# Macaron block, float32, one core: four normalisations on VectorE, the values product at the end of a step, the turned h and h2n in another PSUM bank, SyncE's moves in another order

## What is computed

```python
x = x + 0.5 * ffn_stack(layernorm(x))   # 2 layers: shift_token, qkv of 8 heads of 64,
                                        # l2norm(q), l2norm(k), rotary xpos, attention over
                                        # the own and the previous window of 64, @ wo, residual;
                                        # shift_token, layernorm, w1, a * gelu(g), w2, residual
x = x + attn(layernorm(x))              # z = y @ W for k, q, v; each layernormed with gain and
                                        # bias; softmax(k @ q.T) @ v, over all 1024 tokens; + y
x = x + 0.5 * ffn_stack(layernorm(x))
```

## Time and profile before

| | us |
|---|---|
| median of three runs | 1809.63 (1808.24 to 1811.32) |
| the profiled execution | 1811.45 |
| its span, first to last instruction | 1809.7 |
| granted TensorE clock, mean of the span | 0.967 |

### The profile page before, as it was taken

The page is one execution under the profiler, slowest core; times in us unless marked ns, Lnnn a source line. Parts: engine busy times, 40 slices in busy tenths (PEclk is TensorE's granted clock), DMA queues, the critical chain, the costliest instruction groups (busy, mean ns, idle before and its releaser), DMA issues.

```text
span 1809.7 us, 44041 instructions
## 1 busy us (share of the span) xinstructions
PE 1523.7 (84%) x15864; PEld 1237.8 (68%) x15864; DVE 1323.5 (73%) x3420; ACT 1174.8 (65%) x2460; POOL 1098.1 (61%) x1130
## 2 busy tenths in 40 slices
PE   1789999978999999867878979999998899999984
PEld 1677777766777777754656757777776777777763
DVE  6687879777788887754434469797977687979772
ACT  1576767666677776745565567676766576767671
POOL 3685858576677676633232168585857576858560
PEclk9999999999999999988889989999999999999996
DMA  8241212231312131113100142122223131212113
GB/s 282 49 123 39 59 46 57 55 86 45 77 42 57 40 80 40 41 50 97 35 12 24 33 104 53 44 53 50 55 58 89 41 77 41 58 47 54 44 28 118
DMA packets 183670, 112.46 MB, mean 62 GB/s; under 512 B 86720, under 2 KB 164128, under 8 KB 182944
## 3 DMA queue, kind: packets, MB, share of 16 engines
q1 hardware_dynamic: 183456, 109.65, 23.2%
HBM read 43.41 MB, written 23.42 MB: 37 GB/s over the span
## 4 chain that ended last, share of the span: by engine, by line
PE 51%; DVE 26%; ACT 9%; issue 7%; SPq 3%; DMA 2%; POOL 1%; DVEq 0%; ACTq 0%; POOLq 0%
PE QK L388 10%; PE TO L638 9%; PE QK L638 5%; PE TO L705 5%; DVE rope_c L1136 5%; DVE rope_s L1141 4%; DVE o_n L1161 4%; PE TO L388 3%; DVE top L1080 3%; PE SC L679 3%; DVE h2n L1148 3%; PE TO L807 2%; PE VB L807 2%; PE TO L751 2%; ACT probs L1278 2%
## 5 line engine op out<-in xcount | busy, mean ns | idle before, releaser
L1278 ACT ACTIVATE probs<-SC,shift,qgain 128x128 f32<-128x128 f32 x1024 | 389.7, 480 | 102.2 <-DVE shift L1088 101.9
L1472 POOL TENSOR_TENSOR ve<-mv,epsilon 128x1 f32<-128x1 f32 x128 | 24.3, 190 | 393.4 <-DVE mv L1127 393.4
L388 PE MATMUL QK<-w_qkv,hT 128*128 128x512 f32 x768 | 223.7, 429 | 23.4 <-DMA w_qkv<-qkv_d 10.9
L1136 DVE TENSOR_TENSOR rope_c<-QK,rope 128x512 f32<-128x512 f32 x256 | 175.7, 686 | 81.5 <-PE QK L388 79.0
L1485 POOL TENSOR_TENSOR rnorm<-clip,mhalf 128x8 f32<-128x8 f32 x128 | 210.9, 1647 | 13.1 <-DVE clip L1097 13.1
L1494 POOL TENSOR_TENSOR qgain<-clip,mhalf 128x8 f32<-128x8 f32 x128 | 209.3, 1635 | 0.0
L638 PE MATMUL TO<-ident,probs 128*128 128x128 f32 x1280 | 188.7, 274 | 20.8 <-ACT probs L1278 11.2
L1272 ACT ACTIVATE v_own<-VB 128x512 f32<-128x512 f32 x128 | 76.5, 598 | 191.1 <-PE VB L388 191.1
L1080 DVE TENSOR_REDUCE top<-SC 128x4 f32<-128x512 f32 x256 | 174.6, 682 | 28.8 <-PE SC L679 28.5
L1141 DVE TENSOR_TENSOR rope_s<-QK,rope 128x256 f32<-128x256 f32 x512 | 190.9, 415 | 0.0
L638 PEld LDWEIGHTS TO<-ident,probs 128*128 128x128 f32 x1280 | 152.4, 141 | 54.8 <-issue 34.3
(11 more groups left out here) (170 smaller groups left out, 3760.8 us busy)
## 6 DMA issues: line engine op xcount, KB each, us to landing
v_prev<-v_own SPq DMA_DIRECT2D x256, 130.0 KB, 2.3
x_att<-stream SPq DMA_DIRECT2D x128, 64.0 KB, 2.3
h<-stream SPq DMA_DIRECT2D x256, 32.0 KB, 1.9
stream<-x_new SPq DMA_DIRECT2D x32, 256.0 KB
w_qkv<-qkv_d SPq DMA_DIRECT2D x3, 1536.0 KB, 6.8
h<-x_mid SPq DMA_DIRECT2D x128, 32.0 KB
h<-x_mid SPq DMA_DIRECT2D x128, 31.8 KB
rope<-rope_d SPq DMA_DIRECT2D x24, 128.0 KB, 3.2
```

The costliest lines, as they stand in the source:

```text
L388: last = mm(dst, fr(left(a)), fr(right(b)), start=(k == 0), stop=(k == 2))
L1136: v.tensor_tensor(qk(rope_c[:])[:, m], src, rope[:, i, m, 0:1, :].to_broadcast([P, HEADS, DH]), ALU.mult)
L1278: last = nc.scalar.activation(probs[:, b, hd, :], SC[:, hd * P:hd * P + P], ACT.Exp, bias=shift[:, b, hd:hd + 1], scale=qgain[:, b, hd % 4 ...
```

## The change

- In the preparation of the attention, y's and z's key and query normalisations move from ScalarE to VectorE (eight `tensor_scalar` with mean and rstd each). GpSimd computes only variance plus epsilon and rstd for them (`rstd_of`). The value part stays on ScalarE (`v_normalised`), at stage 7 instead of 8. On VectorE the row's maximum moves ahead of the last of z's additions and its statistics.
- In a stack's step TensorE does the v projection after h's and h2n's turning, before o_n's. h and h2n are turned into the first columns of TT instead of VB. Before the first four probabilities are turned, TensorE waits for s_hl and s_h2l of the step before; the burst's first pair waits for both as well.
- VectorE does the low parts of hT and h2T before the sum of squares.
- ScalarE copies v_own between h2T and oT.
- SyncE moves x_mid into h2 first and v_own into v_prev after that.

```diff
@@ moves, SyncE
-                if t := tile(QKV):
-                    need(sp, s_vown, t.count())
-                    sp.dma_start(v_prev[0:64, k, :], v_own[0:64, k, :]) ...
                 if t := tile(WO):
                     need(sp, s_xm, t.count())
                     sp.dma_start(h2[:, k, 0:64], x_mid[:, i, 0:64]) ...
+                if t := tile(QKV):
+                    need(sp, s_vown, t.count())
+                    sp.dma_start(v_prev[0:64, k, :], v_own[0:64, k, :]) ...
@@ step, TensorE
                     if t := tile(ATT):
+                        if t2 := tile(TH + 1):
+                            pe.wait_ge(s_hl, t2.count())
+                        if t2 := tile(FFN_IN + 1):
+                            pe.wait_ge(s_h2l, t2.count())
                         probs_transposed(t, 0)
...
-                        product(mm, VB[:], lambda x: hT[:, b, x, :], lambda x: w_qkv[:, x, 1024:1536]).then_inc(s_v, 1)
...
-                        transpose(VB[:, 0:P], h[:, t.i % 4, :]).then_inc(s_th, 1)
+                        transpose(TT[:, 0:P], h[:, t.i % 4, :]).then_inc(s_th, 1)
...
-                        transpose(VB[:, P:2 * P], h2n[:, t.i % 2, :]).then_inc(s_th2, 1)
+                        need(pe, s_h2l, t.count(back=1))
+                        transpose(TT[:, P:2 * P], h2n[:, t.i % 2, :]).then_inc(s_th2, 1)
+                    if t := tile(QKV):
+                        b = t.i % 2
+                        need(pe, s_vown, t.count(back=1))
+                        if before is not None:
+                            pe.wait_ge(s_xn, before * 2 + 1)
+                        product(mm, VB[:], lambda x: hT[:, b, x, :], lambda x: w_qkv[:, x, 1024:1536]).then_inc(s_v, 1)
@@ ffn, TensorE
+                    if k == 0:
+                        pe.wait_ge(s_h2l, last_in.count())
+                        if t := tile(TH):
+                            pe.wait_ge(s_hl, t.count())
@@ VectorE
+            def z_normalised(s, m):
+                dve.wait_ge(g_rsk, s * 4 + (2 * m + 2))
+                zz = z_n(s)[:, :, m * DIM:m * DIM + DIM]
+                normalise(zz, zz, KQV + m * TILES).then_inc(g_zn, 1)
+
+            def y_normalised(s):
+                dve.wait_ge(g_rsi, s * 2 + 2)
...
+                normalise(y_n(s), x_m(s), LN_IN).then_inc(g_yn, 1)
@@ rows of the attention, VectorE
                     v.tensor_reduce(nm_g[:, b:b + 1], (QK if b else SC)[:, :], AX, ALU.max, negate=True).then_inc(g_nm, 1)
+                if (s := prepared(g, 1)) is not None:
+                    y_normalised(s)
+                if (s := prepared(g, 5)) is not None:
+                    shifted_in(s, 7)
+                    z_stats(s, 6)
+                    z_stats(s, 7)
+                    z_moments(s)
...
                     v.reciprocal(rl_g[:, b:b + 1], sm_g[:, b:b + 1]).then_inc(g_rl, 1)
+                if (s := prepared(g, 6)) is not None:
+                    z_normalised(s, 0)
...
+                if (s := prepared(g, 6)) is not None:
+                    z_normalised(s, 1)
@@ rows of the attention, ScalarE
-                if (s := prepared(g, 6)) is not None:
-                    z_normalised(s, 0)
-                    z_normalised(s, 1)
-                if (s := prepared(g, 8)) is not None:
-                    z_normalised(s, 2)
+                if (s := prepared(g, 7)) is not None:
+                    v_normalised(s)
@@ GpSimd
+            def rstd_of(slot, n, moments, lot, inverse):
+                own = slice(slot, slot + TILES)
+                pool.wait_ge(moments, n)
+                g.tensor_tensor(ve_g[:, own], mv_g[:, own, 1], epsilon[:, 0:TILES], ALU.add).then_inc(inverse, 1)
+                pool.wait_ge(inverse, 2 * lot - 1)
+                g.tensor_tensor(rs_g[:, own], ve_g[:, own], mhalf[:, 0:TILES], ALU.pow).then_inc(inverse, 1)
```

More of the change, by code:

```diff
@@ L1055, in joined_moments @@
                 stats_fence(g_sti, s + 1)
-                need(dve, g_nbi, s)
+                need(dve, g_rsi, s * 2)
                 aggregate(LN_IN).then_inc(g_mvi, 1)
@@ L1181, in step @@
                     own = slice(t.i * P, t.i * P + P)
-                    v.tensor_tensor(fr(h2T[:, 1, own]), VB[:, P:2 * P], h2T[:, 0, own], ALU.subtract).then_inc(s_h2l, 1)
+                    v.tensor_tensor(fr(h2T[:, 1, own]), TT[:, P:2 * P], h2T[:, 0, own], ALU.subtract).then_inc(s_h2l, 1)
+                if t := tile(QKV):
+                    b = t.i % 2
+                    dve.wait_ge(s_sq, t.count())
+                    need(dve, s_rn, t.count(back=2))
+                    v.tensor_reduce(norm2[:, b, :], sq[:].rearrange("p (h d) -> p h d", d=DH), AX, ALU.add).then_inc(s_n2, 1)
                 if burst == ITERS - 1:
@@ L1292, in step @@
                     exponentials(t, 1)
-                if t := tile(QKV):
-                    b = t.i % 2
-                    act.wait_ge(s_v, t.count())
-                    need(act, s_o, t.count(back=TILES - 1))
-                    if t.c >= 2:
-                        act.wait_ge(s_vlo[b], t.count(back=2, every=2, unit=16))
-                        act.wait_ge(s_vup[b], t.count(back=2, every=2, unit=16))
-                    copy(v_own[:, t.i, :].rearrange("p (h d) -> p h d", h=HEADS)[:, :, 0:DH],
-                         VB[:].rearrange("p (h d) -> p h d", h=HEADS)).then_inc(s_vown, 1)
                 if t := tile(ATT):
@@ L1317, in step @@
                     need(act, s_v, t.count(back=2))
-                    copy(fr(hT[:, t.i % 2, 0, :]), VB[:, 0:P]).then_inc(s_hT, 1)
+                    copy(fr(hT[:, t.i % 2, 0, :]), TT[:, 0:P]).then_inc(s_hT, 1)
                 if t := tile(FFN_IN):
                     act.wait_ge(s_th2, t.count())
-                    copy(fr(h2T[:, 0, t.i * P:t.i * P + P]), VB[:, P:2 * P]).then_inc(s_h2T, 1)
+                    copy(fr(h2T[:, 0, t.i * P:t.i * P + P]), TT[:, P:2 * P]).then_inc(s_h2T, 1)
+                if t := tile(QKV):
+                    b = t.i % 2
+                    act.wait_ge(s_v, t.count())
+                    need(act, s_o, t.count(back=TILES - 1))
+                    if t.c >= 2:
+                        act.wait_ge(s_vlo[b], t.count(back=2, every=2, unit=16))
+                        act.wait_ge(s_vup[b], t.count(back=2, every=2, unit=16))
+                    copy(v_own[:, t.i, :].rearrange("p (h d) -> p h d", h=HEADS)[:, :, 0:DH],
+                         VB[:].rearrange("p (h d) -> p h d", h=HEADS)).then_inc(s_vown, 1)
                 if t := tile(ATT):
@@ L1419, in _ @@
                                          bias=nm_g[:, b:b + 1], accum_out=sm_g[:, b:b + 1]).then_inc(g_p, 1)
-                if (s := prepared(g, 1)) is not None:
-                    y_normalised(s)
                 if (s := prepared(g, 7)) is not None:
@@ L1510, in rstd_and_shift, with kqv_rstd @@
                 g_.tensor_tensor(mn_g[:, own], mv_g[:, own, 0], minus[:], ALU.mult).then_inc(inverse, 1)
-                pool.wait_ge(inverse, 2 * n - 1)
+                pool.wait_ge(inverse, 2 * lot - 1)
                 g_.tensor_tensor(rs_g[:, own], ve_g[:, own], mhalf[:, 0:TILES], ALU.pow).then_inc(inverse, 1)
-                pool.wait_ge(inverse, 2 * n)
+                pool.wait_ge(inverse, 2 * lot)
                 g_.tensor_tensor(nb_g[:, own], mn_g[:, own], rs_g[:, own], ALU.mult).then_inc(shift, 1)
+            def kqv_rstd(s):
+                need(pool, g_zn, s * 2)
+                need(pool, g_vn, s)
+                for m in range(2):
+                    rstd_of(KQV + m * TILES, s * 3 + m + 1, g_mvk, s * 2 + m + 1, g_rsk)
+                rstd_and_shift(KQV + 2 * TILES, s * 3 + 3, g_mvk, s + 1, g_rsv, g_nbv)
             def residual(s):
@@ L1538, in after @@
                 if g == DRAIN + 4:
[L1539 to L1540 removed]
+                    kqv_rstd(0)
             pipeline(step, 0, after)
```

85 lines of the change are left out of this document (30 added, 55 removed).

## The result

| | before | after |
|---|---|---|
| median, us | 1808.93 (1805.35 to 1811.32) | **1843.78** (1839.53 to 1847.62) |
| profiled execution / its span, us | 1811.45 / 1809.7 | 1839.53 / 1837.7 |
| granted TensorE clock, mean | 0.967 | 0.967 |

The ratio is 1.0186 (95% interval 1.0166 to 1.0207). The forecast was 1827, with 1802 to 1846 as its range: the sign was right and the time lies inside the range, 2 us from its end. The loss is 34.9 us where 17.4 had been forecast, twice as much: the mechanism of a regular step came as said, and several of the other terms were mis-sized or missing.

The account below looks back on a forecast made before the run. No engine bounds it, but a 9.18 us step loop through k_r, h2n, o_n and the output product; 26 + 7.5 + 7 − 19 − 2 − 2 = +17.5 on 1811.45 gives 1829, 1827 on the median's base; range 1802 to 1846.

Parts of the forecast that it names:

- The bank: Regular stack steps: the probabilities wait for VectorE's two low-part subtractions; loop grows 0.29 us to 9.47 us, together +26 us.
- rival of unchanged steps: Stack steps: subtractions are done when TensorE arrives, so steps give 0; 1797 us, chance 0.13.
- V product to the end: Stack step: three matmuls, some 0.7 us, move into TensorE's 0.87 us idle before o_n's turning; gain 0.
- v_own's copy: ScalarE in a stack step: copied before oT, which still ends just in time for the output product; nothing on top.
- Bursts: 14 FFN bursts: first pair waits for the same bank and ScalarE's chain comes 0.48 us later; +7.5 us (0 to 12).
- SyncE: Layer changes in both stacks: w_qkv and w_o loads queue behind late v_own's moves; +7 us (0 to 11).
- Attention: Between the stacks: VectorE's normalisations shorten TensorE's waits for keys and y; −19 us, from a gain of 11 to 26.
- its z meets two powers: Drain, first sequence: z's normalisations on VectorE meet two GpSimd powers, so the gain is 0 (−1.5 to +1).
- rival of normalisations held by powers: Attention: each of the 16 normalisation instructions loses to GpSimd, attention gives only 3 us; 1843 us, chance 0.15.
- rival that attention takes all: Attention: ScalarE's relief goes straight to the end (35 us); 1811 us, chance 0.08.
- Escape from GpSimd: Rival, stack steps: k_r starts over 0.1 us after h2n, which runs unheld; loop 0.6 us shorter, about 1745 us, chance 0.04.
- Fill: First steps of a stack: the low part no longer waits behind the sum of squares; −1 each, −2 us.

Follow-up runs that it names:

- A: The changed kernel with hT and h2T copied ahead of the first half's exponentials and both low parts made ahead of the second row maximum; 1795.78 us, ratio 0.9929.
- B: The changed kernel with h2n made by ScalarE instead of VectorE, using one more small product on GpSimd; 1846.72 us, ratio 1.0211.
- the last kernel: The changed kernel with early low parts, h2n on ScalarE, loads ahead of v_own's wait, and the first shift moved behind o_n; 1829.43 us, ratio 1.0100.

## Why the prediction came out as it did

- **The bank, +0.29 a step: right.** 9.47 us was forecast, 9.50 measured; 9.33 after a burst (9.30); the 20 short steps went into the same loop, as said. The wait of TensorE for the low part is in the rows, and its 0.28 us is about what the step grew. A, which takes that wait away, brings the sum of the regular steps back (860.7 against 862.8). It doesn't bring the old steps back: it also moves ScalarE's copies and the second shift, and its steps are 8.8 to 9.75 us. +26 was forecast, +31 came. The rival of unchanged steps wanted the low parts to end at about 411.3; on its scale they ended at 411.57.
- **V product to the end, 0, and v_own's copy, 0: right.** V ran inside the wait for o_n (326.35 to 327.3, o_n at 327.9); moving the copy back changed a step by 0.01 us.
- **Bursts, +7.5: mis-sized, +13.6.** Nine were near the 24.74 us forecast (24.6 to 24.8). Five took 25.9 to 26.3 because the first pair ran at half the clock behind a wait that the change adds. With all at full clock (kernel A) the bursts came to 345.8, 6.9 above before. The forecast had the wait and not what it can do to the clock; that a wait of about the same length left nine bursts at full clock is not explained.
- **SyncE, +7: the sum was near (+9.3), one side of it missing.** w_qkv's load was issued 4.25 us after o_n's turning (394.85, 390.60), with 4.2 forecast, and in the first stack TensorE's wait grew by 1.76 us (1.8), in the second by 2.93. But the step took SyncE's part and the stack's part as one term. Apart they are −13 for h2's loads, freed from the wait for v_own, and +23 for w_qkv and w_o behind a late v_own. The prediction named the first in a sentence and priced it at nothing. The two steps with w_qkv grew by 2.1 and 3.5 us, the two with w_o by 1.7 and 1.9 (1.1 to 2.1 forecast).
- **The six steps at the start and after the FFN's weights, not in the prediction: +6.8.** In the four after the weights (+3.3) x_b2 waits for them, so that k_a, q_r and the low parts come late; with A they are back (37.5 us against 39.5 before and 42.8 after). In the two near the start of the first stack (+3.5) VectorE waits for h2's loads, 3.96 us in the first of them instead of 2.55, behind moves of tables and weights in SyncE's queue; with A they stay long (23.6 us against 20.8 before and 24.3 after).
- **Attention, −19: right at −17.8.** The drain was wrong: −2 for y and 0 for z, where 7.5 came. (The y's part is in the rows, TensorE's wait for it fell from 3.76 to 1.59 us.) The step that failed is "its z meets two powers". No row shows VectorE held by a power: the row of the power at 911.26 says when it ran, not that anything waited. Sixteen normalisations ran beside two powers without loss. That −19 was met so closely is in part luck: its sum has a hold by a power that the traces don't show, and lacks holds that they do show, the two of the first prepared y (2.36 and 2.50 us) and one of 2.38 us in each prepared sequence, by GpSimd's 128x1024 instructions. The rival of normalisations held by powers (1843) is refuted by the sixteen, though its figure came true. The rival that attention takes all asked for −39; the normalisations alone gave −27.
- **Escape from GpSimd (1745), 0.04: the argument against it was right**, and it is worth more than the number. B did what that rival asks for, and q_r held the shift as the prediction says.
- **Fill, −2: open.** The first o_n came 6.4 us earlier, more than the edit can give; kernels that don't touch this code came 2 to 5 us earlier too.

In the profiled executions the span grew by 28.0 us against a sum of +17.5: regular steps +5, bursts +6, loads +2, the six steps +7 and the ends of the stacks and of the kernel +3.5 over the forecast, the interval between the stacks −8 and the start −5.5 under it. The other 7 us of the 17 are the distance of the two profiled executions from their medians (4.3 below it after, 2.5 above it before). The three other executions of the changed kernel had lower granted clocks (0.959 to 0.963, against 0.967 in the profiled one); more bursts at the low clock would do that, but there is no trace of them. The terms that cost more than forecast come to 24 us and those that cost less to 13; without the second kind the time would have been, by these sums, an estimated 1857 us, outside the range. So the range held in part by chance.

The holds can be set beside the Trainium skill (SBUF — State Buffer, "SBUF: two separate sides"), by which the first to start takes the ports that GpSimd and VectorE share for a whole instruction. The trace agrees for k_r, q_r and the product over v that a hold lasts to their end (1.04, 1.27 and 2.35 us). It doesn't agree on who wins, as far as recorded starts show it: in the earlier trace rows h2n started 0.06 us before k_r and was held, which the prediction counts as agreement. And it doesn't agree for the 8-wide powers, which the prediction had weighed by that rule: beside powers of 1.71 and 1.77 us the normalisations went on at 0.26 us each.

## What to carry to other kernels

When one instruction of another engine holds yours, don't ask what the victim costs but when the holder ends, and what stands behind that point: h2n, the first shift and the second shift took turns as victims, and only moving the work that TensorE waited for (the low parts) out from behind the hold paid. In an in-order queue that issues DMAs, read each wait for what is queued behind it, above all at the rare steps with large loads: four steps of 128 held 34 us. And take a change of several parts apart before judging it: here two parts were worth 2.1% together, and the third cost 4% and needed one of them to run at all well.

## What the hardware showed that was not expected

- A 128x8 power on GpSimd of 1.64 to 1.77 us doesn't hold VectorE's SBUF-to-SBUF instructions (16 in 4.19 us), while a 128x512 sum or product of two SBUF operands holds even a 128x4 instruction until it ends, for up to 1.29 us. It doesn't hold everything: in the step shown, the low parts, which read PSUM, and the sum of squares, which reads one SBUF operand, ran beside k_a at 0.29, 0.28 and 1.21 us, and all 107 sums of squares beside k_a in the kernel before took 1.20 to 1.22 us.
- TensorE's clock came at half (0.53 in the window) in 5 of 14 bursts behind idles of 0.68 and 0.99 us and a short turning, and in none of the 56 of the four kernels in which the second idle was gone and the first shift in its place. In the last kernel four of 14 bursts had a stretch at the low clock, but behind the first pair.
- Removing a hold can lengthen a step: 9.50 to 9.71 us, and 9.18 to 9.42 us without the stack's part.
